# Attention scores in 32x32 tiles, attention rows in two PSUM banks, and one earlier load

## What is computed

```python
q, k = rope(x @ Wq), rope(x @ Wk)             # 8 heads of 16
v, g = x @ Wv, x @ Wg                         # 8 heads of 32
scores[h, i, j] = (q_i . k_j) * 16 ** -0.5 * gamma_h ** (i - j)   # j <= i, else 0
o = scores @ v
o = o * rsqrt(mean(o * o, -1) + 1e-5) * g_norm_w
x = layernorm(x + (o.reshape(1, 2048, 256) * silu(g)) @ Wo)
h = silu(fp4(x) @ fp4(w_gate).T) * (fp4(x) @ fp4(w_up).T)         # 352 wide
x = layernorm(x + fp4(h) @ fp4(w_down).T)
```

## Time and profile before

| | |
|---|---|
| median of 3 runs | 134.37 us (134.25 to 134.56) |
| the profiled execution, its own time | 134.68 us |
| its span, first to last instruction | 132.9 us |
| PE, DVE, ACT, POOL busy | 92%, 83%, 67%, 66% of the span |
| mean granted TensorE clock | 0.999 |

### The profile page before, as it was taken

How to read it: one execution, slowest core, us unless ns; L and a number is a source line. 1 busy time by engine, 2 the same in 40 slices (tenths; PEclk the granted TensorE clock), 3 DMA queues, 4 the chain that set the end, 5 groups by cost and what they waited for, 6 DMA issues and landing times.

```text
span 132.9 us, 5148 instructions
## 1 busy us (share of the span) xinstructions
PE 121.9 (92%) x2072; PEld 86.5 (65%) x2072; DVE 109.8 (83%) x329; ACT 88.7 (67%) x311; POOL 87.8 (66%) x124
## 2 busy tenths in 40 slices
PE   4898789999999999999999999899999899999860
PEld 4764447675676576766666577557686688887650
DVE  1239796789689999999999999799999999999810
ACT  3143465573865849576676759687777787899883
POOL 5012443548859667894956688486949797996781
PEclk9999999999999999999999999999999999999999
DMA  3799991000000000000000000000000000010222
GB/s 91 246 282 358 427 435 69 0 7 7 0 5 0 5 5 0 5 2 5 0 7 0 0 5 2 5 5 0 0 5 5 1 21 0 14 50 20 62 79 79
DMA packets 4791, 7.68 MB, mean 58 GB/s; under 512 B 800, under 2 KB 3872, under 8 KB 4512
## 3 DMA queue, kind: packets, MB, share of 16 engines
q1 hardware_dynamic: 3744, 6.60, 14.2%
q10 hardware_dynamic: 1024, 0.76, 1.8%
HBM read 6.31 MB, written 1.05 MB: 55 GB/s over the span
## 4 chain that ended last, share of the span: by engine, by line
PE 73%; DVE 12%; ACT 4%; issue 4%; DMA 3%; POOL 2%; POOLq 0%; DVEq 0%; ACTq 0%
PE ps L313 9%; PE ps L441 7%; PE ps L307 6%; PE ps L421 6%; PE ps L427 6%; PE ps L330 5%; PE ps L355 4%; PE ps L365 4%; PE ps L341 3%; PE ps L301 3%; PE ps L433 3%; PE ps L386 3%; DMA w_qk<-in_w_qk 3%; DVE probs L728 3%; PE ps L387 2%
## 5 line engine op out<-in xcount | busy, mean ns | idle before, releaser
L860 POOL TENSOR_TENSOR rstd_h<-ms,minus_half 128x8 f32<-128x8 f32 x16 | 26.8, 1674 | 7.6 <-DVE ms L744 7.5
L855 POOL TENSOR_TENSOR qk<-rope 128x256 f32<-128x256 f32 x16 | 11.7, 731 | 11.2 <-DVE rope L722 11.2
L313 PE MATMUL ps<-w_vg,xT_sb 128*128 128x512 f32 x32 | 16.7, 604 | 0.5 <-DVE S L739 0.5
L879 POOL TENSOR_TENSOR xq<-x_ratio,xs 128x128 f32<-128x128 f32 x16 | 7.9, 491 | 11.5 <-DVE x_ratio L657 11.5
L722 DVE TENSOR_TENSOR rope<-ps,tabs_sb 128x512 f32<-128x512 f32 x16 | 11.0, 686 | 5.4 <-PE ps L307 5.2
L441 PE MATMUL ps<-wd_T,hT 128*128 128x128 f32 x96 | 14.1, 283 | 1.3 <-DVE r L758 0.7
L871 POOL TENSOR_TENSOR rstd<-veps,minus_half 128x1 f32<-128x1 f32 x16 | 9.3, 581 | 7.7 <-DVE veps L753 7.7
L887 POOL TENSOR_TENSOR hq<-h_ratio,hs 128x352 f32<-128x352 f32 x16 | 13.1, 816 | 1.7 <-DVE h_ratio L657 1.3
L441 PEld LDWEIGHTS ps<-wd_T,hT 128*128 128x128 f32 x96 | 12.1, 191 | 3.1 <-ACT hT L484 1.5
L421 PE MATMUL ps<-wgu_T,xqT 128*128 128x352 f32 x32 | 13.3, 496 | 0.0
L728 DVE TENSOR_TENSOR probs<-ps,causal 128x512 f32<-128x512 f32 x16 | 11.0, 690 | 2.4 <-PE ps L330 2.0
(11 more groups left out here) (110 smaller groups left out, 349.0 us busy)
## 6 DMA issues: line engine op xcount, KB each, us to landing
tabs_sb<-rope_tables SPq DMA_DIRECT2D x1, 2048.0 KB, 12.4
tabs_sb<-rope_tables SPq DMA_DIRECT2D x1, 1280.0 KB, 8.3
out<-x SPq DMA_DIRECT2D x16, 64.0 KB, 1.5
tabs_sb<-rope_tables SPq DMA_DIRECT2D x1, 512.0 KB, 4.3
xT_sb<-x_transposed SPq DMA_DIRECT2D x1, 512.0 KB, 7.9
xT_sb<-x_transposed SPq DMA_DIRECT2D x1, 320.0 KB, 5.6
tabs_sb<-rope_tables SPq DMA_DIRECT2D x1, 256.0 KB, 4.0
w_vg<-in_w_vg ACTq DMA_DIRECT2D x1, 256.0 KB, 4.4
```

What stands on the lines that cost most here:

```text
L313: mm(vg_ps, xT(c), w_vg[:], start=True, stop=True).then_inc(vg_pe, 1)
L855: gp.tensor_tensor(g16(qk[:, c % D, :]), g16(rope[:, c % D, 0, :]), g16(rope[:, c % D, 1, :])[:, :, ::-1, :], ALU.add).then_inc(qk_p, 1)
L860: gp.tensor_tensor(rstd_h[:, c, :], ms[:, c, :], minus_half[:], ALU.pow).then_inc(rms_p, 1)
```

## The change

**Scores.** `scores` makes 16 products where it made 8: the 128 keys are cut in four groups of 32 (`k`) instead of two of 64, so the tiles are 32 rows by 32 columns, all 16 of the array, one product on each, still with 128 elements streamed and into the same places of banks 0 to 3.

**Attention rows.** The rows now lie in banks 1 and 2, one bank for each half chunk `a`, with the two heads of a pair side by side in the bank (columns `CH * e`) on the pair's own 32 partitions. So the products of `from_state` for pair `j` have rows `32j` and columns `32j`: 4 different tiles, four products on each, and the two heads of a pair come one behind the other. Those of `values` still lie on 8 tiles with two on each. The second product on a tile came eight products after the first in both steps; now it comes two after it in `values`, and in `from_state` it is the next one. `start` and `stop` follow the sharing of the bank. `copy_oT`, `squares` and `gated` read or write with the indices in another order, over the same number of elements.

**Banks.** `qkT` moves from bank 0 to 3, `hT` from 3 to 0, `xqT` from 2 to 1, `o` from 1 to 2, the transposed gate and up weights from 3 and 2 to 1 and 0. With rows in banks 1 and 2 only, `transpose_qk` of the next chunk no longer waits for `copy_oT`, only for `mask_scores`.

**Load.** SP issues the load of x for chunks 1 and 2 right behind the tables of chunk 0, no longer behind the wait for them.

**A wait.** `h_ratio_(c)` on DVE waits for POOL's `h_value(c - 6)`, the last reader of the buffer that it overwrites.

**Order.** The lists of PE, ACT, DVE and POOL are written anew. The `warm_up(4)` groups stay in number and behind the same transposes.

```diff
-        BANKS = {"sc": (0, 1, 2, 3), "oT": (0, 1, 2, 3), "o": (1,), "yT": (7,), "qk": (4,), "qkT": (0,),
-                 "vg": (6,), "att": (5,), "xqT": (2,), "gate": (4,), "hT": (3,), "up": (7,),
+        BANKS = {"sc": (0, 1, 2, 3), "oT": (1, 2), "o": (2,), "yT": (7,), "qk": (4,), "qkT": (3,),
+                 "vg": (6,), "att": (5,), "xqT": (1,), "gate": (4,), "hT": (0,), "up": (7,),
...
-        oT_ps = ps[:, 0:4, 0:CH]
-        oT_bank = lambda half, a: ps[:, BANKS["oT"][2 * half + a], 0:CH]
+        oT_ps = ps[:, 1:3, 0:C].rearrange("p a (e q) -> p a e q", q=CH)
+        oT_bank = lambda a, e: ps[:, BANKS["oT"][a], CH * e:CH * e + CH]
...
             load_x(0)
             load_tables(0)
+            load_x(1)
             sp.wait_ge(d_tab[0], 16)
-            load_x(1)
             load_tables(1)
...
-                for a in range(2):
+                for k in range(4):
                     for j in range(NP):
-                        rows = slice(32 * j, 32 * j + 32)
-                        last = mm(sc_ps(j)[CH * a:CH * a + CH, :], kT[rows, c % D, CH * a:CH * a + CH],
-                                  q_eo[rows, c % D, a, :, :].rearrange("p e q -> p (e q)"), start=True, stop=True)
+                        rows, keys = slice(32 * j, 32 * j + 32), slice(32 * k, 32 * k + 32)
+                        last = mm(sc_ps(j)[keys, :], kT[rows, c % D, keys],
+                                  q_eo[rows, c % D, k // 2, :, :].rearrange("p e q -> p (e q)"), start=True, stop=True)
...
                 for a in range(2):
                     for n in range(NH):
-                        j, e, slot32 = n // 2, n % 2, n % 4
+                        j, e = n // 2, n % 2
                         rows = slice(32 * j, 32 * j + 32)
-                        mm(oT_bank(n // 4, a)[32 * slot32:32 * slot32 + 32, :],
-                           S[rows, (2 * c + a) % 8, e * DV:(e + 1) * DV], q_eo[rows, c % D, a, e, :], start=True, stop=False)
+                        mm(oT_bank(a, e)[rows, :], S[rows, (2 * c + a) % 8, e * DV:(e + 1) * DV],
+                           q_eo[rows, c % D, a, e, :], start=e == 0, stop=False)
...
-                        last = mm(oT_bank(n // 4, a)[32 * slot32:32 * slot32 + 32, :],
-                                  v_sb[keys, c % D, n * DV:(n + 1) * DV], probs[keys, c % D, n, :], start=False, stop=True)
+                        last = mm(oT_bank(a, e)[32 * j:32 * j + 32, :],
+                                  v_sb[keys, c % D, n * DV:(n + 1) * DV], probs[keys, c % D, n, :], start=False, stop=e == 1)
...
-            state_product(0); scores(0); project_vg(1); from_state(0); values(0); state_product(1); project_qk(2)
-            transpose_qk(1); warm_up(4); transpose_o(0); project_vg(2); scores(1); project_vg(3); from_state(1)
+            state_product(0); scores(0); project_vg(1); from_state(0); values(0); project_qk(2); transpose_o(0)
+            state_product(1); transpose_qk(1); warm_up(4); project_vg(2); scores(1); project_qk(3); project_vg(3)
...
-            def h_ratio_(c): quant_ratio(h(c), sh(c), blocks(h_ratio[:, c % 6, :]), hquant_v, c)
+            def h_ratio_(c):
+                if c >= 6:
+                    dve.wait_ge(hq_p, c - 5)
+                quant_ratio(h(c), sh(c), blocks(h_ratio[:, c % 6, :]), hquant_v, c)
```

More of the change, by code:

```diff
@@ L457, in _ @@
             transpose_y(5); project_vg(8); project_qk(10); transpose_xq(3); up(2); scores(7); out_projection(5)
-            from_state(7); state_product(8); values(7); gate(3); transpose_o(7); transpose_qk(8); transpose_y(6)
+            from_state(7); state_product(8); values(7); transpose_qk(8); gate(3); transpose_o(7); transpose_y(6)
             project_vg(9); project_qk(11); transpose_xq(4); up(3); scores(8); out_projection(6); from_state(8)
@@ L470, in _ @@
-            transpose_qk(14); transpose_h(0); transpose_y(12); project_vg(15); up(9); transpose_xq(10)
-            out_projection(12); scores(14); gate(10); state_product(15); from_state(14); values(14); transpose_y(13)
-            down(0); transpose_o(14); transpose_h(1); transpose_qk(15); up(10); out_projection(13); transpose_xq(11)
-            down(1); scores(15); gate(11); up(11); from_state(15); values(15); transpose_y(14); transpose_o(15)
-            transpose_h(2); transpose_xq(12); out_projection(14); gate(12); transpose_h(3); up(12); down(2)
@@ L475, in _ @@
-            transpose_h(4); transpose_y(15); down(3); transpose_h(5); out_projection(15); down(4); transpose_h(6)
-            transpose_xq(13); down(5); gate(13); transpose_h(7); down(6); up(13); transpose_h(8); transpose_xq(14)
-            down(7); gate(14); transpose_h(9); up(14); down(8); transpose_h(10); transpose_xq(15); down(9); up(15)
+            transpose_xq(8); out_projection(10); scores(12); gate(8); state_product(13); from_state(12); values(12)
+            transpose_qk(13); transpose_y(11); transpose_o(12); project_vg(14); transpose_xq(9); up(8); scores(13)
@@ new lines, in _ @@
+            gate(9); out_projection(11); from_state(13); state_product(14); values(13); transpose_h(0)
+            transpose_qk(14); transpose_o(13); transpose_y(12); project_vg(15); up(9); transpose_xq(10)
+            out_projection(12); scores(14); gate(10); from_state(14); state_product(15); values(14); transpose_qk(15)
+            transpose_y(13); down(0); transpose_o(14); transpose_h(1); up(10); out_projection(13); transpose_xq(11)
+            down(1); gate(11); scores(15); up(11); from_state(15); values(15); transpose_y(14); transpose_h(2)
@@ L902, in _ @@
[L902 to L906 removed]
+            rotate_add(5); rotate_add(6); rms_rstd(3); gated_output(3); ln1_rstd(2); rotate_add(7); x_value(1)
```

209 lines of the change are left out of this document (106 added, 103 removed).

## The result

The changed kernel took **141.5 us** (141.17 to 141.79, four runs) where the kernel before took 134.47 us beside it (134.25 to 134.88). The ratio is 1.0518, with a 95% interval from 1.0479 to 1.0558: it is slower by 7 us. I had predicted slower, and 136.0 us; the time lies above the range of 133.2 to 139.8.

What follows compares the result with a forecast made beforehand. PE, busy 92%, was taken as the bound. Terms 2.64 + 0.5 - 0.3 - 0.4 - 0.4 - 0.4 made +1.6 us on the profiled 134.68, 136.3; median 0.3 lower: 136.0 us, range 133.2 to 139.8.

Steps and rivals of the forecast that it cites:

- (2): `scores` as 16 products on 16 tiles, one on each: +0.03 us a chunk, between -0.03 and +0.06.
- (1): `from_state` with four products on each of 4 tiles: 0.57 us for 0.38, +0.19 a chunk (0.15 to 0.24).
- (3): `values`: +0.05 us behind `state_product` in 10 of chunks 4 to 15 (0 to +0.15); alone unchanged at 0.38.
- (4): The start, up to `scores(4)`: the reordered work brings it -0.3 us, between -0.9 and +0.4.
- (5): Banks and order: fewer `copy_oT` waits, -0.4 us; `state_product`'s wait covered, -0.4; for both between +1 and -1.5.
- (6): The tail: `h_ratio_(10)` moved ahead of the last mask brings -0.4 us, between -0.6 and 0.
- (7): The wait in `h_ratio_`, other index orders and the early load of x: 0 us; the load 0 to +0.3.
- A: Whole kernel not slower: new lists take away PE's remaining idle time; 133.5 us, or 132.5; chance 0.20.
- B: Whole kernel: as A, but a third of it, within 0.3 us of before, 134.3 us; chance 0.10.
- C: `from_state` and `values`: a product held by its tile holds those behind it; 158 us, chance 0.04; milder form 139.2.
- D: `from_state`: pairs take turns at a bank, +0.66 us a chunk, 143.5 us; chance 0.05.
- E: `scores`: 16 tiles don't run side by side, two rounds, +0.22 us a chunk, 139.5; 0.11 with C's mild form.

## Why the prediction was wrong

**The direction** was right: `from_state` on 4 tiles costs some 2.6 us in the middle, and there was little idle time on PE to hide it in.

**The step that failed is "the change part by part" (2)**, the finer scores at +0.03 us a chunk. As PE's own time that is right (0.035). But I counted only the time of the 16 more MATMUL rows a chunk, and put two things at nothing without a reason. First, that they are instructions that have to be brought: the stops cost 3.1 us in `values` and 0.4 in `scores`. Second, that the mask waits for the last of the 16 products: it started 0.11 us later in a chunk, where the step that PE does next started 0.03 later; I had gone by the distance from one of PE's rows to the next alone. Why it is 0.11 no run shows. Taking the finer scores out again gave back 4.6 us. Nothing in the sum, the bounds or the rivals stood for it. The page of the kernel before had what was needed to ask about the first, 16 packets of 16 KB of instructions:

```profile
q8 instruction: 16, 0.26, 0.8%
```

**(1) from_state, mis-sized.** +0.19 predicted (0.15 to 0.24), +0.235 measured. The count of four products on the fullest tile was right; interleaved, it costs +0.195, as the sum had it. The other 0.04 comes from the order, two heads of a pair one behind the other; that the fourth tile then gets its first product later is a likely reason, not a measured one. **(3) values, mis-sized**: +0.05 behind `state_product` predicted, +0.08 measured, and alone +0.05 where I had 0. Together (1) to (3) are 3.8 us in eleven chunks instead of 2.9.

**(4) The start, -0.3 predicted, +0.16 measured.** `scores(1)` at 16.34 (16.1 predicted), `from_state(1)` at 18.26 (18.3), `scores(4)` at 35.27 (34.8). Without the finer scores it is 16.07 and 34.63 (-0.48), so the reordering gives what I said. The changed kernel's profile lost 0.27 us by `scores(1)`, where PE waited 1.5 us for the state behind `wgu_nat` instead of 0.6, 0.25 by the small stop in chunk 2, and 0.1 by the later mask of chunk 3.

**(5) Banks and lists, -0.8, half of it right.** With the scores in 8 products the middle is 68.67 - 65.63 = 3.04 us longer, and its steps explain 11 x 0.235 + 3 x 0.05 + 8 x 0.08 = 3.4. The rest is `state_product`'s wait, which a longer `from_state` covers as I had said: 3 x 0.13 = 0.4 us. The other 0.4 isn't there. PE's weight loads waited for `copy_oT` 2.8 us in 10 waits between 35 and 104 us before and 0.5 us in 2 after, as forecast, but the middle isn't shorter for it; which other waits took their place I didn't take apart.

**(6) The tail, -0.4: right.** 31.82 us for 32.20 from `scores(15)` on, with `h_ratio_(10)` (L649, 128x352) ahead of the last mask, as the earlier trace rows had them the other way round:

```profile
108.12 0.53 DVE L649 SCALAR_TENSOR_TENSOR h_ratio<-h_blocks,hs 128x352 f32<-128x352 f32 x1
108.86 0.69 DVE L729 TENSOR_TENSOR probs<-ps,causal 128x512 f32<-128x512 f32 x1 [0.22 <-PE ps L330]
```

**(7) At nothing**: the load of x was right by two runs, though it delayed `wgu_nat`, which I hadn't listed; the wait of `h_ratio_` wasn't tested alone.

**The rivals.** A and B are out: steps grew by more than idle time could cover. C is out: `from_state` is 0.62 us, not 1.5, and in the interleaved order only 0.04 less; its mild form, +0.2 in `values`, is out at +0.05 to 0.08. The Trainium skill's rule (TensorE: Matmul & The Clock Gate, Part 3, The mechanism), on which C rested, thus doesn't describe products on different tiles here: 32 rows of 56 ns that waited for each other would be 1.8 us. D is out: `from_state` with four pairs' rows in one bank takes 0.62 us, 0.58 in the other order, where turns at a bank would need 1.04. E is out: 16 tiles ran side by side, 0.43 us in all.

**The sum by what was measured**, from `scores(4)` to `scores(15)`: the stops 3.1 and 0.25, the later mask 0.9 (the finer scores stood in my sum with 0.33 for eleven chunks), `from_state` and `values` 3.4, `state_product`'s wait -0.4, makes 7.25 of 7.28 us; +0.16 before it and -0.38 behind it complete the 7.1.

**What stays open**: what decides at which step the transfer of a packet begins. It began at the same step in several chunks running and then moved to another; with the finer scores inside the run it came as late as 1.3 us before PE reached a packet's end, with the same rows outside it didn't. The runs show the consequence, not the rule. Open are also the two stops of 0.2 us in `scores` and why the mask comes 0.11 us later.

## What to carry to other kernels

Count the instructions of an engine before cutting its work finer, ask when the engine that waits for the result can start, and look at the queue of instructions in the page. Where a stretch of many short instructions takes less time than a packet takes to come, a stop of about a microsecond can fall into any of them, the profile calls it "issue", and equal distances in numbers of instructions (not in time) give it away; a few idle instructions ahead of it, which move it, prove it. And for products on small tiles count the rows on the fullest tile, 56 ns each for float32, before their length.

## What the runs showed of the hardware

- PE's instructions came in packets of 16 KB, 125 or 126 MATMUL rows with their weight loads. When it had used up what it had, PE went on 2.2 to 2.8 us after the next packet's transfer began, in `values`, `state_product` and `scores` of ten runs; the longest stop, 3.1 us, is one where the transfer began only when PE was already standing. The Trainium skill (Runtime: NRT & Kernel Launch, Instruction fetch mechanics) has the blocks of 16 KiB and 256 instructions, with which the trace agrees, and says that their fetch is hidden since instructions are issued more slowly than they arrive; here the trace disagrees, with stops of 0.7 to 1.2 us in runs of small products.
- A float32 MATMUL row on a 32x32 tile takes 56 ns of that tile with 2 streamed elements and as many with 64; on four tiles in turn 56 such rows took 0.92 us, on one 3.14.
- 16 tiles of 32x32 run side by side: 32 rows with 128 streamed elements in 0.43 us.
- The reader of 16 products on 16 tiles started 0.68 us after the first of them, that of 8 products of the same length on 8 larger tiles 0.57 us.
